# Value projection of a sliding-window attention block from seven quarter products, and rope products written back into PSUM

## What is computed

```python
qkv = x @ w_qkv.T                      # 16 heads of 32
q, k = rope(q), rope(k)                # pairs (even, odd) of a head's columns
scores = einsum(q, k) * scale, kept where 0 <= row - column < 64, else -inf
x = layernorm(x + (softmax(scores) @ v) @ w_out.T)
gate = silu((x @ w_gate) * s_gate); up = (x @ w_up) * s_up      # int8 weights, 512 -> 2048
x = layernorm(x + ((gate * up) @ w_down) * s_down)              # 2048 -> 512
```

## Time and profile before

| | |
|---|---|
| median of 3 runs | 1167.48 us (1166.87 to 1167.51) |
| span of the profiled execution | 1164.2 us |
| PE busy | 1154.0 us (99%) |
| DVE busy | 984.6 us (85%) |
| ACT busy | 584.4 us (50%) |
| POOL busy | 587.3 us (50%) |

### The profile page before, as it was taken

One profiled execution on the slowest core, in us unless ns is written; L12 is line 12 of the kernel. 1 busy time (PEld: TensorE's weight loads), 2 busy tenths in 40 slices (PEclk: granted clock), 3 DMA queues, 4 the chain that ended last, 5 costly groups with the idle time before them and its releaser, 6 DMA issues.

```text
span 1164.2 us, 25539 instructions
## 1 busy us (share of the span) xinstructions
PE 1154.0 (99%) x8433; PEld 567.9 (49%) x8433; DVE 984.6 (85%) x2821; ACT 584.4 (50%) x1640; POOL 587.3 (50%) x563
## 2 busy tenths in 40 slices
PE   9999999999999999999999999999999999999998
PEld 4344446444464444644455444554445444464444
DVE  7899998898987899879998899897898988986434
ACT  3953883048820588105880169701686027950330
POOL 0775684156731667326771367613676236752330
PEclk9999999999999999999999999999999999999999
DMA  9999786366562765617656096561964537734000
GB/s 295 173 175 252 137 166 160 66 88 137 111 149 55 110 131 107 145 41 128 132 97 141 37 146 119 101 132 46 155 123 88 131 63 137 120 73 109 19 2 36
DMA packets 352077, 134.80 MB, mean 116 GB/s; under 512 B 309840, under 2 KB 332496, under 8 KB 351952
## 3 DMA queue, kind: packets, MB, share of 16 engines
q1 hardware_dynamic: 334976, 106.86, 49.6%
q0 software_dynamic: 10560, 17.30, 5.1%
q10 hardware_dynamic: 6416, 9.00, 2.1%
HBM read 32.19 MB, written 8.39 MB: 35 GB/s over the span
## 4 chain that ended last, share of the span: by engine, by line
PE 97%; DVE 1%; ACT 1%; issue 1%; POOL 0%; POOLq 0%; DVEq 0%
PE bank L842 61%; PE bank L1058 18%; PE bank L848 10%; PE bank L984 3%; PE bank L964 2%; PE bank L864 1%; PE bank L1080 1%; ACT bank L1243 1%; PE bank L873 0%; PE bank L1069 0%; PE bank L948 0%; DVE wd L1373 0%; ACT wu L1186 0%; DVE ffn_tmp L1530 0%; ACT fuse L1186 0%
## 5 line engine op out<-in xcount | busy, mean ns | idle before, releaser
L842 PE MATMUL bank<-x1T,wg 128*128 128x512 f16 (+1 forms) x1032 | 242.5, 378 | 0.0
L842 PE MATMUL bank<-x1T,wu 128*128 128x512 f16 x1024 | 241.9, 379 | 0.0
L1243 ACT ACTIVATE bank<-bank,neg_max,qk_scale 128x128 f32<-128x128 f32 x512 | 220.5, 435 | 7.8 <-DVE neg_max L1558 6.1
L1058 PE MATMUL bank<-wd,fuse 128*128 128x512 f16 (+2 forms) x1056 | 222.7, 373 | 0.0
L660 POOL TENSOR_TENSOR fuse<-ffn_tmp,fuse 128x512 f16<-128x512 f32 x128 | 149.7, 1170 | 117.5 <-ACT fuse L1186 116.8
L742 POOL TENSOR_TENSOR fuse<-fuse 128x512 f16<-128x512 f32 x116 | 137.7, 1218 | 74.9 <-ACT fuse L1186 72.8
L1058 PEld LDWEIGHTS bank<-wd,fuse 128*128 128x128 f16 x1056 | 101.9, 98 | 118.0
L842 PEld LDWEIGHTS bank<-x1T,wu 128*128 128x128 f16 x1024 | 100.1, 98 | 120.7
L655 POOL TENSOR_TENSOR xT_sb<-probs,xT_sb 128x512 f16<-128x512 f32 x112 | 129.6, 1158 | 44.5 <-ACT xT_sb L1186 44.4
L842 PEld LDWEIGHTS bank<-x1T,wg 128*128 128x128 f16 x1032 | 96.3, 98 | 113.9 <-issue 4.0
L1196 ACT ACTIVATE ffn_tmp<-bank,tanh_scale 128x512 f32<-128x512 f32 x128 | 88.2, 689 | 100.0 <-PE bank L842 76.8
(11 more groups left out here) (235 smaller groups left out, 1621.5 us busy)
## 6 DMA issues: line engine op xcount, KB each, us to landing
v_cross<-v_own SPq DMA_DIRECT2D x64, 128.0 KB, 2.4
out<-x ACTq DMA_DIRECT2D x31, 256.0 KB, 2.0
xT_sb<-xT SPq DMA_DIRECT2D x30, 256.0 KB, 4.1
qkT<-x SPq DMA_DIRECT2D x28, 256.0 KB, 3.8
wg<-w_gate POOLq DMA_DIRECT2D x7, 1024.0 KB, 5.2
wu<-w_up POOLq DMA_DIRECT2D x7, 512.0 KB, 6.0
wqkv<-w_qkvT SPq DMA_DIRECT2D x8, 256.0 KB, 6.3
wg<-w_gate POOLq DMA_DIRECT2D x1, 2048.0 KB, 8.4
```

The source lines that it names most:

```text
L842: last = pe.matmul(dst, lhsT, rhs, start=(i == 0), stop=(i == len(pairs) - 1))
L1058: last = pe.matmul(dst[:, cols], fuse[:, s, z, rows], wd[:, s, cols], start=(s == 0 and z == 0), stop=(s == STEPS - 1 and z == 1))
L1243: last = act.activation(unit, unit, ACT.Exp, bias=neg_max[:, s % 2, h // 3, h % 3:h % 3 + 1], scale=qk_scale[:, 2:3], accum_out=row_sum[:, ...
```

## The change

1. Values of tiles 1 to 7 are made like queries and keys: two pairs of blocks, of each seven quarter products of 256 columns (2 f32 matmuls each), 14 quarters in place of 16 matmuls of 512 columns. Three are issued at the end of a body (`begin_values`), eleven at the head of the next (`project_values`).
2. The products are added in another way, for queries, keys and values: PE accumulates the next product onto the one that is in the bank, and between the two ACT copies out what stands there. So sixth waits for the copy of first, seventh for the copy of sixth, fourth for the copy of seventh. ACT has four copies of 512 columns for a pair of queries and keys (one before), and eight of 256 columns for the values of a tile. DVE has three additions a pair (seven before), and four `add_v` a tile.
3. `keep_v` and `split_v` read the finished values from SBUF (`v_rows`) in place of PSUM. Gate products 0 and 1 wait for `add_v(1)` and `add_v(3)`.
4. In loop tiles two of the four rope products are written back into the bank that they are read from, and `rope_sums` reads them there. The next user of the bank waits for `rope_done` in place of `rope_read`.
5. The added weights of the values are made once by POOL in the prologue, written to DRAM (three DMAs of 256 KB), and read back into a part of `v_cross` once a body by a DMA on ACT's queue (`load_v_weights`). POOL in the prologue also makes the sums for blocks 0 and 1 of tile 1.
6. Orders at the heads of the lists change, and so does the end of the prologue on PE.

The core of the diff, engine by engine:

```diff
 # PE: a body's head
-                    project_v(a, 1, ffn)
-                    project_v(a, 2, ffn)
-                    scores(a, 0, ffn)
-                    scores(a, 1, ffn)
-                    project_v(a, NB - 1, ffn)
+                    project_values(a)
...
-                        wait(v_low, pe, a, 2 * s + 1)
+                        wait(v_added, pe, a - 1, 2 * s + 1)
...
-                    project_v(a + 1, 0, ffn)
+                    begin_values(a + 1)
...
+            def project_pair(a, i):
...
+                pair_first(a, i)
+                wait(x_summed, pe, a - 1, 7)
+                pair_fifth(a, i)
+                pair_sixth(a, i)
+                pair_second(a, i)
+                pair_seventh(a, i)
+                pair_third(a, i)
+                pair_fourth(a, i)
...
+            def begin_values(a):
+                values_first(a, 0)
+                values_fifth(a, 0)
+                values_first(a, 1)
+
+            def project_values(a):
+                values_sixth(a, 0)
+                values_third(a, 0)
+                values_fifth(a, 1)
+                values_seventh(a, 0)
+                values_sixth(a, 1)
+                values_second(a, 0)
+                values_fourth(a, 0)
+                values_third(a, 1)
+                values_seventh(a, 1)
+                scores(a, 0, True)
+                scores(a, 1, True)
+                values_second(a, 1)
+                values_fourth(a, 1)
 # PE: the prologue's end
-                        project_v(a + 1, 0, True)
-                project_pair(a + 1, 1, True)
+                        pair_second(a + 1, 1)
+                wait(proj_read, pe, a, 2)
+                pair_first(a + 1, 1)
+                project_o(a, NB - 1, ffn)
...
+                pair_fifth(a + 1, 1)
+                pair_sixth(a + 1, 1)
+                pair_third(a + 1, 1)
+                pair_seventh(a + 1, 1)
+                pair_fourth(a + 1, 1)
+                begin_values(a + 1)
 # ACT: a body's head
+                    keep_values_first(a, 0)
+                    keep_values_fifth(a, 0)
+                    keep_values_first(a, 1)
+                    keep_values_sixth(a, 0)
+                    keep_values_fifth(a, 1)
+                    keep_values_seventh(a, 0)
+                    keep_values_sixth(a, 1)
+                    split_high(a, 2, ffn)
+                    keep_values_seventh(a, 1)
+                    split_high(a, 3, ffn)
                     keep_v(a, 0, ffn)
-                    split_high(a, 2, ffn)
                     keep_v(a, 1, ffn)
+                    exponentials(a, 0, ffn)
                     keep_v(a, 2, ffn)
-                    split_high(a, 3, ffn)
-                    exponentials(a, 0, ffn)
                     keep_v(a, NB - 1, ffn)
                     exponentials(a, 1, ffn)
 # ACT: what the first of them waits for, and the prologue's end
+            def keep_values_first(a, i):
+                if i == 0:
+                    wait(pair_summed, act, a - 1, 3 * turn_of(1) + 2)
...
+                keep_first(a + 1, 1)
                 for j in range(2):
                     split_x1_high(a, j, ffn)
                 split_high(a + 1, 1, True)
-                keep_first(a + 1, 1)
+                keep_fifth(a + 1, 1)
+                keep_sixth(a + 1, 1)
+                keep_seventh(a + 1, 1)
                 carry_v(a + 1)
 # ACT: a body's end
+                keep_seventh(a + 1, 0)
                 keep_first(a + 1, 1)
                 split_high(a + 1, 0, ffn)
+                keep_fifth(a + 1, 1)
+                keep_sixth(a + 1, 1)
+                split_high(a + 1, 1, ffn)
+                keep_seventh(a + 1, 1)
                 carry_v(a + 1)
-                split_high(a + 1, 1, ffn)
 # DVE: front
+                    add_v(a, 0)
+                    add_v(a, 1)
                     for j in range(2):
                         split_v(a, j, ffn)
                     for s in range(2):
                         maxima(a, s, ffn)
                         bias(a, s)
+                    add_v(a, 2)
+                    add_v(a, 3)
+                    weights(a, 0, ffn)
                     split_v(a, 2, ffn)
-                    weights(a, 0, ffn)
                     split_v(a, NB - 1, ffn)
                     weights(a, 1, ffn)
 # DVE: rope
-                    i = (0, 3, 1, 2)[part]
+                    i = ((3, 0, 1, 2) if ffn else (0, 3, 1, 2))[part]
...
+                    dst = src if ffn and part % 2 else place[i]
...
+                even, odd = qk_banks(j, ffn) if ffn else (place[0], place[2])
...
+                dve.tensor_tensor(place[0], even, place[1], ALU.subtract)
+                done(rope_done, dve.tensor_tensor(place[2], odd, place[3], ALU.add))
 # POOL: the prologue
                 sum_w(3)
+                sum_first_x(0)
                 split_low(a + 1, 0, True, range(2))
                 invert_deviation1(a, 2)
                 split_low(a + 1, 0, True, range(2, 4))
+                lessen_v_weights()
+                add_v_weights()
+                keep_v_weights()
```

More of the change, by code:

```diff
@@ L533, in cross_v @@
             def cross_v(a, j):
+                if j == 0 and not (isinstance(a, int) and a == 0):
+                    wait(v_product[1], sp, a - 1, V_FOURTH)
+                    sp.sem_inc(passed, 1)
+                    sp.wait_ge(v_weights_kept, 3 * 16)
+                    sp.sem_inc(passed, 1)
                 wait(v_low, sp, a, j)
@@ new lines, in lessen_v_weights, with add_v_weights @@
+            def lessen_v_weights():
+                low_left, low_right, high_left, high_right = v_quarters()
+                wait(v_done, pool, 0, NB - 1)
+                pool.tensor_tensor(low_right, low_right, low_left, ALU.subtract).then_inc(v_weights_lessened, 1)
+            def add_v_weights():
+                low_left, right_less_left, high_left, high_right = v_quarters()
+                second, third, fourth = (added_v_weights(n) for n in range(3))
+                wait(pv_done, pool, 0, STEPS - 1)
+                pool.wait_ge(v_weights_lessened, 1)
+                pool.tensor_tensor(second, high_right, right_less_left, ALU.subtract).then_inc(v_weights_added, 1)
+                pool.wait_ge(v_weights_added, 1)
+                pool.tensor_tensor(fourth, high_left, second, ALU.subtract).then_inc(v_weights_added, 1)
+                pool.tensor_tensor(third, second, low_left, ALU.subtract).then_inc(v_weights_in[0], 16)
@@ L839, in _, with product, quarter @@
         def _(pe):
-            def product(dst, pairs):
+            def product(dst, pairs, onto=False):
                 for i, (lhsT, rhs) in enumerate(pairs):
-                    last = pe.matmul(dst, lhsT, rhs, start=(i == 0), stop=(i == len(pairs) - 1))
-                return last
+                    last = pe.matmul(dst, lhsT, rhs, start=(i == 0 and not onto), stop=(i == len(pairs) - 1),
+                                     skip_group_check=onto)
+                return last
+            def quarter(dst, lhsT, rhs, onto=False):
+                return product(dst, [(lhsT[:, k, :], rhs[:, k, :]) for k in range(KC // 2)], onto)
             def qkv(j, part, dst, parts=range(KC)):
@@ L878, in project_odd, with pair_first @@
                     done(qk_done, last)
-            def project_pair(a, i, first=False):
-                front_even, front_odd, back_even, back_odd = pair_banks(i)
+            def pair_first(a, i):
                 front_low, front_high, back_low, back_high = x_quarters(i)
                 low_even, odd_less_even, high_even, high_odd = w_quarters()
-                sums, turn = x_sums(i), turn_of(i)
-                def quarter(dst, lhsT, rhs):
-                    return product(dst, [(lhsT[:, k, :], rhs[:, k, :]) for k in range(KC // 2)])
+                done(first_product, quarter(pair_banks(i)[2], front_low, low_even))
@@ L915, in project_v, with values_first @@
-            def project_v(a, j, ffn, parts=range(KC)):
+                wait(*((proj_read, pe, a - 1, NB - 1) if i == 0 else (down_read, pe, a - 2, NB - 1)))
+                pair_first(a, i)
[6 more added lines that the diff above has]
+                pair_fourth(a, i)
+            def values_first(a, i):
+                front_low, front_high, back_low, back_high = x_quarters(i)
+                low_left, right_less_left, high_left, high_right = v_quarters()
+                wait(rope_done, pe, a, i)
+                done(v_product[i], quarter(v_places(i)[3], front_low, low_left))
@@ L957, in scores @@
                 elif ffn:
-                    wait(rope_read, pe, a, 2 if s == 0 else NB - 1)
+                    wait(rope_done, pe, a, 2 if s == 0 else NB - 1)
                 for h in range(HG):
@@ L1311, in body @@
                         keep_probs_high(a, s - 1, ffn)
+                    if attn and s == 0:
+                        wait(v_low, act, a, 1)
                     gate_tanh(f, s)
@@ L1331, in body @@
```

(3 more changed lines are left out.)

288 lines of the change are left out of this document (173 added, 115 removed).

## The result

The changed kernel took 1201.1 us (median of 4 runs, 1199.99 to 1202.59) where the one before took 1167.17 us beside it (4 runs, 1165.75 to 1167.51): ratio 1.0292, 95% interval 1.0279 to 1.0306. The forecast was 1187.8 us with a range up to 1198. So the sign was right and the forecast wait is there, but the loss was 34 us instead of 20, and most of it stands at other places (table). The profiled execution has a span of 1200.8 us, 36.6 more than before; the forecast had 20.3.

What follows compares the result with a forecast made beforehand. PE's own instructions were taken to bound the kernel. Span 1164.2 + 13.4 (six loop tiles) + 6.9 (tile 1: 4.7 prologue, 2.2 head) = 1184.5, plus 3.3 to the median: 1187.8 us; forecast's own range 1172 to 1196, whole range 1168 to 1198.

Steps and rivals of the forecast that it cites:

- That adds 0.1: Behind a body's head: scores(6), needing weights(3) at S + 21.7 against S + 21.65, adds 0.1 us a tile.
- the 3.3 us between span and median: Whole kernel: the median of the runs was taken to lie 3.3 us above the profiled span, giving 1187.8 from 1184.5.
- Quarters, 1.83 us a tile: Values on PE: fourteen quarters take 12.10 us for 13.93 before, a gain of 1.83 us a tile, 12.8 for seven.
- Copies between the quarters, rope in place, 0: Loop tiles: ACT's copies between accumulating products are covered and in-place rope is free; bounds 0 to 1 us a tile, taken 0.
- The head, +2.13 us: Head of a body: PE stands 3.9 us for add_v(3), so gate product 1 comes 2.13 us later than before.
- Prologue, 4.7: Prologue's end: late copies and DVE's chain bring scores(0) of tile 1 later, taken as 4.7 us, bounds 1.5 to 7.
- The full saving: Rival at the body's head: DVE is not held at split_v(0), the quarters' saving arrives, 1156 us; chance 0.13.
- Copies too late everywhere: Rival in queries', keys' and values' products: copy cover used up, 1.5 us a tile or more extra, 1198 and up; chance 0.10.
- the sign given for it: Sign in loop tiles: PE waits inside project_pair would show the forecast wrong, the time then near 1198.
- Quarters save nothing: Rival on PE: accumulating onto a bank just read costs what fewer columns save, 1188 + 12.8 = 1201; chance 0.03.

Runs made afterwards that it cites:

- e7: Changed kernel with the edits of e1, e2 and e6 together: 1165.61 us, ratio 0.9990 to the kernel before.
- e5: Kernel before with only the in-place rope products of loop tiles, without the quarters of values: 1170.05 us, ratio 1.0025.
- e2: Changed kernel with ACT's loop cut to repeat behind the FFN steps, no longer between tail and head: 1202.51 us, ratio 1.0301 to the kernel before.
- e3: Changed kernel with the edits of e1 and e2 together: 1169.21 us, ratio 1.0026 to the kernel before.
- e1: Changed kernel with keep_v(0) and keep_v(1) on ACT ahead of the copy of seventh(1) and split_high(3): 1173.58 us, ratio 1.0053 to the kernel before.
- e4: Kernel before with one wait added on PE, gate product 1 waiting for bias(2) on DVE: 1199.74 us, ratio 1.0278.
- e12: Kernel before with a shorter wait added on PE, gate product 1 waiting for fused(0): 1181.3 us, ratio 1.0126.
- e9: e1 with the second step's probabilities split ahead of the FFN's part on ACT and POOL: 1174.08 us, ratio 1.0057 to the kernel before.
- e6: Changed kernel with the order at the prologue's end altered on POOL, ACT and DVE: 1199.65 us, ratio 1.0280 to the kernel before.
- e10: e8 with the second step's probabilities turned on SP ahead of the last copies of values: 1165.99 us, ratio 0.9996 to the kernel before.
- e8: e7 with the second step's probabilities split ahead of the FFN's part on ACT and POOL: 1165.88 us, ratio 0.9981 to the kernel before.
- e11: e7 with only SP's order altered, the second step's probabilities turned ahead of the last copies of values: 1166.4 us, ratio 0.9994 to the kernel before.

## Why the prediction was wrong in size, by its steps

By the spans the forecast had 20.3 us more and the run 36.6. The step that failed is the check behind the head, "That adds 0.1": it followed the late weights to `scores(6)` alone, past the DMA for the second `weigh_v`, and took PE to come back from its idle at full speed. It had 0.7 us for seven tiles, and the run has 9.5. Next is the prologue, 9.6 for 4.7, then the 0 for the copies (4.0), and tile 4 (2.2). The head, 3.7 us too dear, hid a part of this. So did the 3.3 us between span and median: the profiled execution after was the slowest of its four, and the median lies only 0.3 above it. In medians the miss is 13.3 us and not 16.3, and that is luck.

- **Quarters, 1.83 us a tile.** Right within a tenth: 1.70 at the mark of gate products 0 and 1, 12.0 in all in e7.
- **Copies between the quarters, rope in place, 0.** Right in the loop for the copies of queries and keys and for rope (e5), wrong in one place. The first copy of values comes 1.6 us late, as ACT's loop repeats there (e2). Of the 4.0 us that this stretch cost, 2.4 are PE's waits for it, and e2 and e3 give back 2.6 and 2.5; the other 1.4 to 1.5 stay when the wait is gone, about 0.3 us a tile, most of it at the same product, with no wait that the profile names (0.17 us ahead of it and 0.10 behind its first matmul in tile 3 of e2). What they are is open. I checked what ACT does ahead of the copy in its list, not that the list ends just there.
- **The head, +2.13 us.** The mechanism and the chain were right to 0.03 us up to `keep_v(0)`; e1 shows it by undoing it. The size was 1.62, 0.5 less, since of the two splits one was slowed, not both: 0.69 and 1.64 against 2.71 for the pair. Minus 3.7 in all. Both can be slow: tile 1 of e2 has 1.58 and 1.64 and gate product 1 at S + 10.52.
- **"That adds 0.1."** The step that failed most: 9.5 us instead of 0.7. I had `weights(1)` right and then followed it only to scores(6), the next product that needs DVE. Two things were left out. The second `weigh_v` needs the same weights first, by way of ACT, POOL and a DMA from SP: 0.97 us where PE came there on time (tile 4; with small waits +1.16, and +1.13 in tile 6), and in e1 this stretch is 0.5 to 1.3 longer in the seven tiles. And PE does not come back from an idle at full speed: 1.69 us behind each wait of e4, 1.48 to 1.69 in tiles 2, 3, 5 and 7. They don't add up, as PE that is late by the clock finds the probabilities there. So the clock added about 0.5 us in each of four tiles to what the other wait would have cost there. That most of the 9.5 would have come without the clock is an estimate from e1, where the granted clock behind gate product 1 is 1.00 and the stretch still has 7.1 us more in all.
- **Prologue, 4.7.** It was 9.6. PE is 1.3 us late at 87 us already, ahead of anything changed on its path; executions of one and the same prologue differ by 1.1 (the kernel before, e4, e12), and with the changed order S of tile 1 is at 124.6 to 126.4 (after, e1, e2, e3, e9). Then, against the starts of before: 1.35 at the first product of the pair, 0.85 at fourth, 4.2 at the first accumulating product of values, 1.7 in the two slow ones behind it (2.07 and 1.80 us for 1.03 each), 0.2 in small gaps. I had 0.3 at third, which did not come, 0.9 at fourth, and 3.3 for the values: 0.9 too little. Missing were the slow products, and this, that PE comes 1.7 us sooner to the pair's product that waits (the values of block 0, 3.63 us, have moved behind it, and the second product, 1.92, ahead), and finds its bank still read:

```profile
94.98 1.98 PE L903 MATMUL bank<-wqkv,xT_sb 128*128 128x512 f32 x4 [1.28 <-DVE x L1763]
...
107.98 1.98 PE L903 MATMUL bank<-w_sums,xT_sb 128*128 128x512 f32 x4 [0.69 <-ACT v_own L1324]
```

- **Tile 4, 2.2.** POOL stood idle for 7.17 us ahead of a DMA issue (655.01) and made a row statistic late, and a down product waited 1.87 us for what DVE does behind it. POOL's idle at this issue is in every version, 4.57 in the kernel before and 4.6 to 5.4 in the others, and costs them 0 to 0.4 us; the 2 us more are this execution's.
- **The rivals.** The full saving is ruled out by 22.7 us of waits. "Copies too late everywhere" had the right time (1198 and up) by luck: not ten tight places in a tile were late but one, for 2.4 us in all, and the sign given for it, PE waits inside `project_pair` of loop tiles, did not come. "Quarters save nothing" had 1201, and e7 shows that they save.

The Trainium skill (SBUF — State Buffer, Who interferes with whom) says that the port pair shared by VectorE and GpSimd is an exclusive lock, where issue order decides who blocks. That speaks against counting every instruction beside POOL as slow, as I did; the trace agrees in that of two neighbouring splits under the same POOL work one took 0.69 and the other 1.64 us, and in that one addition took 1.17 us in some executions and 4.42, to the end of POOL's row, in others (e6). For the loop's edge, the Trainium skill (Runtime: NRT & Kernel Launch, Instruction fetch mechanics) says that a taken branch out of the fetched pages makes the engine wait for the target page. The trace shows the 5.10 us of "issue", and e2 that the late copy goes with the cut of the loop; neither shows what they are spent on.

## What to carry to other kernels

Work that is taken from the bound engine just before a place where it depends on others must be followed to every later consumer of the late engine, by way of its DMAs, and not only to the next one. Price a new idle of that engine with what it does to its clock: here 2.9 us of idle cost 4.6, and 1.6 us cost 1.6 to 1.7. Before a small saving is believed, look at more than one execution of the same order: here one addition beside POOL moved a mark by some 3 us. Look where each engine's loop repeats before its first instruction becomes one that another waits for, and test a small wait only where no larger one stands behind it.

## What the runs showed of the hardware

- TensorE's granted clock after an idle: behind 2.87 us it fell to a mean of 0.72 over the next 6 us in all of tiles 2 to 7 of e4, and tiles 2 to 6 lost the same 1.69 us; behind 1.59 us it stayed at 1.00 (e12); behind 3.2 us it fell in four tiles of seven (after), and behind the 3.1 us of e12's tile 1 it did not; behind 2.12 us in the prologue of e5 it was 0.72. So the length of the idle alone does not tell. In tile 4 of e2 it was 0.51 over 6 us, that is, almost all of it at 1.2 GHz.
- ACT's loop repeat: 5.1 us in which its next copy did not start though its product was done for 1.6 of them (after, tile 3).
- DVE's split with f32 and f16 inputs from SBUF: the one of block 1 took 1640 to 1645 ns in all seven tiles beside POOL, the one of block 0 0.69 to 0.71 us, beside POOL too (after).
- DVE's addition of two f32 inputs from SBUF beside four POOL instructions: 1.17 us (e6, e7, e10) or 4.42 (e8, e11), where POOL's four then took 4.50 us and not 5.05.
- SP: the pair of copies of values between the two turns held its queue for 1.7 to 2.5 us in tiles 2 to 6 (e7, e9), where it took 1.2 in the kernel before, and a turn that was ready stood behind them (e9: split done at 422.88, turn issued at 425.94).
